# A changed order of work in the slots of the first layer, on all engines

## What is computed

```python
x = x + _L0_attn_ref(_L0_cond_ref(x, fside, fside, embed, itok_B_0_5), w_qkv, b_qkv, w_out, b_out)
x = x + _L0_ffn_ref(_L0_cond2_ref(x, itok_B_0_63, W, b), w_gate, w_up, w_down)
...
# _L0_cond_ref: softmax((x + embed[stage]) @ f.T) @ f, over the 256 tokens of a sequence
# _L0_attn_ref: 16 heads of 16 features, rotated q and k, causal softmax, projection
# _L0_cond2_ref: x @ W[cat_id] + b[cat_id], one matrix for each sequence
def _L0_ffn_ref(x, w_gate, w_up, w_down):
    gate = fp4_linear(x, w_gate)      # fp4_linear quantises x and w in blocks of 16 ...
    y = fp4_linear(x, w_up)
    h = jax.nn.silu(gate) * y         # ... so h (704 wide) is quantised too
    return fp4_linear(h, w_down)
def fp4_quant_dequant(x):
    scale = max(max(abs(block)) / 6, 1e-12)
    return nearest_of(0, .5, 1, 1.5, 2, 3, 4, 6)(block / scale) * scale
```

## Time and profile before

| what | value |
|---|---|
| median of 3 runs | 2461.85 us |
| the profiled execution's own time | 2440.37 us |
| its span, first to last instruction | 2438.6 us |
| mean granted TensorE clock | 0.982 |
| PE, DVE, ACT, POOL busy in the stretch 100 to 700 us | 547.4, 474.4, 395.0, 280.6 us |
| first layer, steady turns | about 100 to 700 us |

### The profile page before, as it was taken

One profiled execution on the slowest core, in us unless ns is written; L12 is line 12 of the kernel. 1 busy time (PEld: TensorE's weight loads), 2 busy tenths in 40 slices (PEclk: granted clock), 3 DMA queues, 4 the chain that ended last, 5 costly groups with the idle time before them and its releaser, 6 DMA issues.

```text
span 2438.6 us, 53844 instructions
## 1 busy us (share of the span) xinstructions
PE 2262.9 (93%) x18368; PEld 2057.9 (84%) x18368; DVE 1840.2 (75%) x5132; ACT 1291.7 (53%) x3839; POOL 1005.2 (41%) x1063
## 2 busy tenths in 40 slices
PE   4788989999887799999999999899999999999999
PEld 3677878778776688888888887799999999999999
DVE  5778787777878666666666665588868888888876
ACT  1666666666663455555555555434325555555522
POOL 5435445354444455555555554133322222222073
PEclk8999999999998899999999999899999999999999
DMA  4523323233240312212212113131226767777443
GB/s 138 177 87 102 107 88 109 86 99 107 82 129 3 82 38 56 51 44 56 50 45 57 47 47 85 28 79 36 45 73 226 233 229 234 237 230 236 146 121 124
DMA packets 196341, 259.23 MB, mean 106 GB/s; under 512 B 58646, under 2 KB 168486, under 8 KB 185318
## 3 DMA queue, kind: packets, MB, share of 16 engines
q1 hardware_dynamic: 187206, 237.13, 32.0%
q0 software_dynamic: 8864, 18.66, 3.0%
HBM read 176.10 MB, written 43.94 MB: 90 GB/s over the span
## 4 chain that ended last, share of the span: by engine, by line
PE 61%; DVE 15%; ACT 8%; POOL 7%; issue 6%; DMA 1%; POOLq 0%; SPq 0%; DVEq 0%; ACTq 0%
PE bank L55 51%; PE bank L136 6%; ACT Ph L654 2%; POOL P L1786 2%; ACT Ph L656 2%; PE bank L1296 1%; DVE Ph L815 1%; ACT PTh L666 1%; PE bank L1336 1%; DVE xe L921 1%; DVE sgs L945 1%; PE bank L399 1%; POOL Qn L1811 1%; POOL Qn L1809 1%; DVE hb L955 1%
## 5 line engine op out<-in xcount | busy, mean ns | idle before, releaser
L1490 ACT ACTIVATE P<-P,mx 128x144 f32<-128x144 f32 x512 | 206.2, 405 | 263.8 <-DVE mx L1611 262.9
L55 PE MATMUL bank<-xD_hi,w1e_lo 128*128 128x256 f32 x880 | 251.1, 285 | 0.0
L2623 POOL DMA_INDIRECT xE<-d_y,ixs x78 | 111.2, 1426 | 336.3 <-PE bank L136 300.8
L55 PE MATMUL bank<-w2e_hi,hrD_hi 128*128 128x256 f32 x880 | 249.0, 283 | 0.0
L55 PE MATMUL bank<-w2e_lo,hrD_hi 128*128 128x256 f32 x880 | 248.9, 283 | 0.0
L55 PE MATMUL bank<-w2e_hi,hrD_lo 128*128 128x256 f32 x880 | 248.9, 283 | 0.0
L1786 POOL TENSOR_TENSOR P<-P,rs 128x512 f32<-128x512 f32 x128 | 133.1, 1040 | 273.9 <-DVE rs L1620 270.4
L55 PE MATMUL bank<-xD_lo,w1e_hi 128*128 128x256 f32 x880 | 245.9, 279 | 0.0
L55 PE MATMUL bank<-xD_hi,w1e_hi 128*128 128x256 f32 x880 | 245.6, 279 | 0.0
L2232 ACT ACTIVATE hD<-bank,b1E 128x256 f32<-128x256 f32 x312 | 127.0, 473 | 197.2 <-PE bank L55 188.1
L1120 POOL TENSOR_TENSOR xe<-xe 128x704 f32<-128x704 f32 (+3 forms) x64 | 88.2, 1378 | 340.5 <-DVE xe L926 340.3
(11 more groups left out here) (324 smaller groups left out, 7922.3 us busy)
## 6 DMA issues: line engine op xcount, KB each, us to landing
w1raw<-in_ew SPq DMA_DIRECT2D x39, 1024.0 KB, 6.0
w2raw<-in_ew SPq DMA_DIRECT2D x39, 1024.0 KB, 4.9
stack<-d_rot SPq DMA_DIRECT2D x256, 96.0 KB, 2.7
K<-Kn SPq DMA_DIRECT2D x256, 72.0 KB, 2.1
d_rot<-QKh SPq DMA_DIRECT2D x64, 256.0 KB, 3.1
Q<-Qn SPq DMA_DIRECT2D x256, 64.0 KB, 2.0
d_ys<-oE SPq DMA_DIRECT2D x39, 256.0 KB, 2.6
d_rot<-QKl SPq DMA_DIRECT2D x32, 256.0 KB, 2.9
```

The source lines that it names most:

```text
L55: inst = e.matmul(out, l, r, start=k == 0, stop=k == len(pairs) - 1)
L1490: inst = e.activation(P1[t % 2][:, n, :], P1[t % 2][:, n, :], ACT.Exp, bias=mx1[t % 2][:, 2 * g + sg:2 * g + sg + 1], scale=-1.0, accum_ou ...
L2623: e.indirect_dma_start(out=xE[q % 2][c], out_offset=None, in_=d_y, in_offset=bass.IndirectOffsetOnAxis(ap=ixs[r % 4][:, c:c + 1].bitcast(U ...
```

## The change

The slots keep their eight steps of heads; other calls move between slots or change places within one. No operation is added or left out.

- PE: in slot 0 `first_values` and `turn_sums` go ahead of `values`, and `spread_sums` behind `turn_heads`; in slot 5 `turn_category` goes ahead of `first_scores`.
- ACT: in slots 1 to 4 `copy_turned` goes ahead of `exps`; in slot 3 `hidden_high` too; `heads_high(b+1, 0)` moves from slot 1 to slot 3 and `heads_high(b+1, 1)` from slot 3 to slot 4, in each case behind `exps` of the slot (b = -1 stays as it was).
- DVE: the two products `multiply(·, 1, ·)` move from slot 0 into slot 7 of the turn before, between the passes of `hidden_steps`; the second `hidden_steps` moves from slot 1 to slot 0, ahead of slot 1's `maxima`; `category_quant` moves ahead of slot 4's `maxima`, `hidden_low` ahead of `add_category`, `category_low` ahead of `first_max`; `invert_sums` behind the passes.
- POOL: the second `rounded` of h moves from slot 2 to slot 1, ahead of the rotations; `heads_low(b+1, 0)` moves from slot 2 to slot 3, `heads_low(b+1, 1)` from slot 3 to slot 4.

```diff
 # pe_ab
                     scores(P + 1)
+                    if p == 0:
+                        first_values(b + 1)
+                        turn_sums(b - 1)
                     if p % 2 == 0:
                         values(P // 2 - 1)
-                    if p == 0:
-                        turn_sums(b - 1)
-                        first_values(b + 1)
-                        spread_sums(b - 1)
...
                     turn_heads(P)
+                    if p == 0:
+                        spread_sums(b - 1)
...
                     if p == 5:
+                        turn_category(b - 1)
                         first_scores(b + 2)
-                        turn_category(b - 1)
 # act_ab
                         first_copy(b + 1)
+                        x1_high(b + 1)
                         sums_copy(b - 1)
-                        x1_high(b + 1)
...
+                    if 1 <= p <= 4:
+                        copy_turned(P)
+                    if p == 3:
+                        hidden_high(b - 2, 1)
                     exps(P + 1)
                     if p == 1:
                         hidden_high(b - 2, 0)
-                    if p == 3:
-                        hidden_high(b - 2, 1)
...
-                    copy_turned(P)
-                    if p == 1:
+                    if not 1 <= p <= 4:
+                        copy_turned(P)
+                    if p == (1 if b == -1 else 3):
                         heads_high(b + 1, 0)
-                    if p == 3:
+                    if p == (3 if b == -1 else 4):
                         heads_high(b + 1, 1)
 # dve_ab; steps() and hidden_steps() get parts=(0, 1, 2), the passes to run
-                    if p == 0:
-                        multiply(b - 2, 1, 0)
-                        multiply(b - 2, 1, 1)
...
                     if p == 6:
+                        category_low(b - 1)
                         first_max(b + 2)
-                        category_low(b - 1)
...
+                    if p == 4:
+                        category_quant(b - 1)
                     maxima(P + 1)
...
                         hidden_scales(b - 2, 1)
-                        if b == B + 1:
-                            hidden_steps(b - 2, 1)
                         x1_low(b + 1)
+                        hidden_steps(b - 2, 1)
                     if p == 1:
                         turn_qk(b + 1, 0)
                         normal_out(b - 1)
-                        if b <= B:
-                            hidden_steps(b - 2, 1)
                         hidden_low(b - 2, 0)
...
                     if p == 3:
+                        hidden_low(b - 2, 1)
                         add_category(b - 1)
-                        hidden_low(b - 2, 1)
-                    if p == 4:
-                        category_quant(b - 1)
...
                         gated(b - 1, 1, 1)
+                        multiply(b - 1, 1, 0)
+                        hidden_steps(b - 1, 0, (0,))
+                        multiply(b - 1, 1, 1)
+                        hidden_steps(b - 1, 0, (1, 2))
                         invert_sums(b)
-                        hidden_steps(b - 1, 0)
 # pool_ab
-                    if p == 2 and 0 <= b - 2 < B:
+                    if p == 1 and 0 <= b - 2 < B:
                         rounded(quant_of(b - 2, 2), 128, FFN)
...
+                    if p == (2 if b == -1 else 3):
                         heads_low(b + 1, 0)
                     if p == 3 and b >= -1:
                         first_query(b + 2)
-                    if p == 3:
+                    if p == (3 if b == -1 else 4):
                         heads_low(b + 1, 1)
```

More of the change, by code:

```diff
@@ L913, in scales, with steps @@
                 e.reciprocal(rs, m).then_inc(*vs.up())
-            def steps(i, P, W, src):
+            def steps(i, P, W, src, parts=(0, 1, 2)):
                 nb = W // 16
@@ L919, in steps @@
                 x, s = xn[i % 2][0:P, 0:W], ex[i % 2][0:P, 0:W]
[L920 to L926, removed]
+                if 0 in parts:
+                    e.wait_ge(s_v, vs.n)
+                    e.scalar_tensor_tensor(out=x.rearrange("p (n k) -> p n k", k=16),
+                                           in0=src.rearrange("p (n k) -> p n k", k=16),
+                                           scalar=1.0 - 2.0 ** -23, in1=r3, op0=ALU.mult, op1=ALU.mult).then_inc(*vs.up())
+                if 1 in parts:
+                    e.wait_ge(s_v, vs.n)
+                    e.tensor_scalar(s.bitcast(U32), x.bitcast(U32), 0x7F800000, None, ALU.bitwise_and).then_inc(*vs.up())
+                if 2 in parts:
+                    e.wait_ge(s_v, vs.n)
+                    e.tensor_scalar(s, s, 1.0, MAGIC, ALU.max, ALU.mult).then_inc(v_st, 1)
             def category_quant(b):
@@ L962, in hidden_scales, with hidden_steps @@
                 scales(quant_of(b, 1 + st), 128, FFN, hb[st])
-            def hidden_steps(b, st):
+            def hidden_steps(b, st, parts=(0, 1, 2)):
                 if not 0 <= b < B:
                     return
-                steps(quant_of(b, 1 + st), 128, FFN, hb[st])
+                steps(quant_of(b, 1 + st), 128, FFN, hb[st], parts)
             def hidden_low(b, st):
```

## The result

The changed kernel takes 2572.57 us, the median of 4 runs (2570.60 to 2575.49), against 2459.87 for the kernel before beside it: a ratio of 1.0464, 95% interval 1.0440 to 1.0488. That is 113 us more, where the prediction said 54 and a range that ended at 2536. The direction and the main mechanism were right; the size was twice the one forecast.

A forecast was written before the change was run, and what follows sets the result against it. The prediction took PE to bound the first layer, busy 547.4 of 600 us. 14 turns x 2.4 us lost (34), plus 14 x 1.7 for the clock (24), less 4, made +54: 2516 us, range 2456 to 2536.

The forecast's parts named there:

- Slots 3 to 5: One chain behind `category` over four engines: `turn_category` after 15.45 us, not 12.71; with `first_scores`, 4.5 lost per turn.
- L931 and L934: Forecast sign: these DVE passes of the category, held by POOL, take about 1 us rather than 0.43.
- The first four slots: Waits go and `project(b+1, 1)` starts earlier, so `category` comes 1.7 us earlier per turn (bounds 1.0 and 3.0).
- the 0.65 of the prediction: Between `project(b+1, 1)` and `category`: the wait for hq goes, winning 0.65 us.
- The clock: PE idle ahead of `turn_category` brings a spell at half clock: 1.7 us per turn, taken between nothing and 3.4.
- The 4 that turns 0 and 15 were to give back: Turns 0 and 15 have the gain without the chain and give back some 2 us each.
- Twice the spell: Rival: the half-clock spell lies all outside PE's idle piece, 48 us for the clock; +78, 2540 us; chance 0.12.
- The faster case: Rival: chain stays hidden, `turn_category` waits for nothing (below 2 us the change wins); -32, 2430 us; chance 0.11.

The follow-up runs named there:

- e4: Changed kernel with 24 unread matmuls on PE ahead of `turn_category`'s wait for hq: 2527.58 us, ratio 1.0271 to the kernel before.
- e1: Changed kernel with `heads_high` and `heads_low` back in their old slots: 2480.72 us, ratio 1.0081 to the kernel before.
- e2: Changed kernel with `category_quant` back behind slot 4's `maxima` on DVE: 2489.08 us, ratio 1.0113 to the kernel before.
- e12: Changed kernel with `project(b+1, 1)` ahead of `values(4b)` on PE: 2556.03 us, ratio 1.0372 to the kernel before.
- e11: Changed kernel with ten unread matmuls ahead of `values(4b)`'s wait for OT: 2550.84 us, ratio 1.0353 to the kernel before.
- e6: Kernel before with only `copy_turned` (copies to PTh) ahead of `exps` in slots 1 to 4: 2451.81 us, ratio 0.9979.
- e10: e9 with `project(b+1, 1)` ahead of `values(4b)` on PE: 2442.87 us, ratio 0.9911 to the kernel before.
- e13: e10 with the second gate product between the quantiser's passes in slot 7, `invert_sums` kept early: 2449.28 us, ratio 0.9936 to the kernel before.
- e9: e6 with `category` ahead of `turn_hidden(b-2, 1)` on PE: 2437.45 us, ratio 0.9919 to the kernel before.

## Why the prediction was half of it

The turn by stretches, from the rows above, against the terms of the prediction (us; e4 shows the same turn with the clock whole):

| stretch | before | forecast | after | e4 |
|---|---|---|---|---|
| start of b to `category` | 18.28 | -1.70 | +1.49 | -0.01 |
| `category` to `turn_category` | 12.71 | +2.74 | +3.01 | +3.07 |
| `turn_category` to `scores(8b+7)` | 0.36 | +1.73 | +2.94 | +1.67 |
| from there to the next start | 11.93 | -0.30 | +0.16 | -0.23 |
| the clock, apart | | +1.70 | in the rows above | none |
| sum | 43.28 | +4.17 | +7.60 | +4.50 |

**Slots 3 to 5: right.** Link by link the chain is as forecast: to `add_category` 371.11 - 369.18 = 1.93 (1.93), maxima to exps 0.67 (0.66), exps to the copy 378.99 - 377.22 = 1.77 (1.77), `rounded` 384.85 - 381.11 = 3.74 (3.80). The quantiser took 376.63 - 371.84 = 4.79 against 2.93 + 1.6, so DVE was held for 1.86 us. Held were not L931 and L934, as the prediction said it would show (0.43 each), but L915, 1.26 in place of 0.18, and L926, 1.47 in place of 0.69, which came under POOL's L1115 and L1094. `first_scores` behind `turn_category` cost its 1.7, by e4. That the loop needs both edits, e1 and e2 show.

**The first four slots: the step that failed.** The prediction had `project(b+1, 1)` start as soon as `turn_qk` ended, 322.2 - 311.40 = 10.8 us into the turn. `turn_qk` did end about then: the rows of DVE after the change have it at 409.86 + 1.40 = 411.26, 10.97 into the turn.

```profile
409.86 1.40 DVE L879 SCALAR_TENSOR_TENSOR rot0s<-bank,b_qk,rot 128x512 f32<-128x512 f32 x2
411.18 0.68 DVE L837 TENSOR_TENSOR OT<-bank,OT 128x512 f32<-128x512 f32 x1
```

But ahead of `project` on PE stands `values(4b)`, and it needs a second thing beside PTh: the bank that `normal_out` empties, and `normal_out` stands behind `turn_qk` on DVE. Before the change that was hidden: OT was done at 320.61 + 0.68 = 321.29, and `values` waited until 322.57 for PTh. After it PE goes on only at 412.01, when OT is done, works 0.79 on `values`, and comes to `project` at 412.80, 1.54 later than DVE alone would allow. In e4, where the clock is out of it, `project` starts 396.12 - 383.61 = 12.51 into the turn against 323.36 - 311.40 = 11.96 before; the rest of the stretch gained 0.56, near the 0.65 of the prediction; together nothing. The 1.7 us per turn were never there. The mistake is one of reading: the view of waits had put `values` down to the last of its releasers, PTh, and the next one was not looked for. e12 adds that reordering PE would not have saved the gain: `values` moves behind `project`, and in place of OT PE waits 0.8 for rot0s.

**The clock: right in kind, too small.** 1.7 us were taken for one fall per turn; in most turns there were two, and e4's period is 50.88 - 47.78 = 3.1 shorter. One spell of 3.4 us costs 1.35 at the wait for hq (e11), and the second one 1.6 in the changed kernel (50.9 against 49.3), so the price per fall was not too low, the number of falls was. The Trainium skill, page TensorE: Matmul & The Clock Gate, section HAM oscillation — how this bites in real kernels, has the loop in which each turn's wait brings the clock down again; the 19 spells agree with it in that the falls recur in every turn. The page puts them down to one wait in each turn, and there the runs differ: the hq wait of 3.67 us is followed by a fall in the changed kernel and one of 3.70 in e11 is not, the OT wait of 1.39 is and the one of 1.40 in e4 is not. Filling one of the two waits in a turn did away with falls at the other too, all but one in e4, a part in e11. Yet one doesn't need the other: in e1, without a wait for hq, nine of twelve waits for OT are followed by a fall. So what the clock costs is shown, and that filling a wait brings it back; by what rule it falls stays open.

**The sum.** Over 14 turns the misses are 1.69 + 0.33 - 0.06 + 0.07 and 3.10 - 1.70 for the clock, 3.4 in all: 48 us of the 59 between 54 and 113. The 4 that turns 0 and 15 were to give back did not come: the first `category` starts 1.4 later than before (115.79 against 114.41), and 4.8 are lost from the one of turn 15 to the one of turn 16. What these ends of the layer cost, some 7 in all, was not taken apart further.

**The rivals.** Twice the spell was the nearest, with about the right clock loss (3.4 forecast, 3.1 measured) for another reason. The faster case fell at its own point: `turn_category` waits 3.8 us, not under 2. e6, e10 and e13 show besides that it would have won little: of a wait that is taken away most comes back at the next one.

## What to carry to other kernels

Before a wait is counted as won, list everything that the waiting instruction needs, and when each comes under the new order; the view of waits names only the last. Then do the same for the next instruction that waits: in e6 29.5 us of waits were worth 5, and in e9 letting work that needs nothing go ahead was worth three times that. An edit that is harmless alone can close a loop with another, so look for the engine that now stands in two chains at once (here DVE's maxima, between the quantiser and the heads). Where TensorE waits in every turn, price the clock by a run with unread matmuls in the gap: it separates the wait from what the clock adds.

## What the runs showed of the hardware

The granted clock fell behind waits of only 1.39 us, also where no longer wait of PE stood in the turn (e1); it stayed whole behind waits of 1.66 before the change and behind one of 3.70 in e11. So in these runs the length of a wait doesn't say by itself whether the clock falls. In the changed kernel, filling 10 or 24 unread matmuls into one of the two gaps removed falls at the other as well. A spell of 3.4 us cost 0.4 us of the turn in e1 and 1.35 in e11. Matmuls that do nothing made a kernel 45 us faster (e4). DVE's small pass on 128x32 took 1.26 us while POOL's L1115 ran, and the one with two operands in SBUF, L926, 1.47 beside L1094; the end of L915 at 373.82 is that of L1115 at 373.78, while L926 ends 0.54 behind L1094, as if it had done most of its 0.69 only then. The Trainium skill, page SBUF — State Buffer, section Who interferes with whom, has these two engines share a pair of ports that only one of them holds at a time, for a whole instruction; the rows agree.
